# Two-layer attention kernel: three products of the context's values at other places in the first sequence's start

## What is computed

```python
def xattn(Q, K, V, valid_lens, Wq, Wk, Wv, Wo):
    q, k, v = heads(Q @ Wq), heads(K @ Wk), heads(V @ Wv)
    S = einsum('bhqd,bhkd->bhqk', q, k) / sqrt(dh)
    S = where(mask, S, -1e20)
    return merge(softmax(S) @ v) @ Wo

def ffn(h, ...):
    pooled = h.mean(axis=1)
    logits = relu(pooled @ gw1.T + gb1) @ gw2.T + gb2
    top_vals, top_idx = top_k(logits, 2); gates = softmax(top_vals)
    q, k, v = (svd_moe(h, p) for p in 'qkv')   # h @ Wm.T + experts + bias
    return svd_moe(merge(softmax(q k^T) @ v), 'o')

x = x + xattn(layernorm(x), ctx, ctx, lens, Wq, Wk, Wv, Wo)
x = x + ffn(layernorm(x), ...)
```

## Time and profile before

| | us |
|---|---|
| median of three runs | 1447.97 |
| lowest and highest | 1446.61, 1449.62 |
| profiled execution | 1451.72 |
| its span, first to last instruction | 1449.9 |
| its mean granted TensorE clock | 0.971 |

### The profile page before, as it was taken

One profiled execution on the slowest core, in us unless ns is written; L12 is line 12 of the kernel. 1 busy time (PEld: TensorE's weight loads), 2 busy tenths in 40 slices (PEclk: granted clock), 3 DMA queues, 4 the chain that ended last, 5 costly groups with the idle time before them and its releaser, 6 DMA issues.

```text
span 1449.9 us, 17120 instructions
## 1 busy us (share of the span) xinstructions
PE 1397.0 (96%) x5688; PEld 700.9 (48%) x5688; DVE 952.5 (66%) x1687; ACT 862.0 (59%) x1499; POOL 681.1 (47%) x411
## 2 busy tenths in 40 slices
PE   6999999999999999999999999999999999899886
PEld 4545544544454554545455554545455554444332
DVE  4464577767766777767766777767767676766532
ACT  2426474866487664866578663866577663756441
POOL 2022143556455462546446462545446462567463
PEclk9989989999999999999999999999999999999967
DMA  6533233522533224522523224522423222422300
GB/s 213 155 108 95 50 69 102 136 74 49 141 80 91 71 58 116 150 75 45 136 76 104 70 57 118 150 74 45 125 83 103 74 54 80 132 59 55 77 28 29
DMA packets 78239, 130.81 MB, mean 90 GB/s; under 512 B 26358, under 2 KB 31094, under 8 KB 75079
## 3 DMA queue, kind: packets, MB, share of 16 engines
q1 hardware_dynamic: 74055, 128.66, 33.2%
q10 hardware_dynamic: 4096, 1.06, 0.3%
HBM read 66.08 MB, written 12.21 MB: 54 GB/s over the span
## 4 chain that ended last, share of the span: by engine, by line
PE 86%; ACT 5%; DMA 2%; issue 2%; POOL 2%; SPq 1%; DVE 1%; ACTq 0%; POOLq 0%; DVEq 0%
PE pj L1099 43%; PE scT L1184 9%; PE acc L1213 8%; PE sc L1156 7%; PE sc L1145 3%; PE pj L1129 2%; PE scT L1177 2%; PE pj L1193 2%; PE pj L1201 2%; PE pj L1222 2%; PE pj L1093 2%; ACT xhat L707 1%; PE pj L1074 1%; ACT qs L790 1%; PE pj L1085 1%
## 5 line engine op out<-in xcount | busy, mean ns | idle before, releaser
L822 ACT ACTIVATE probs<-scT 128x512 f32<-128x512 f32 x512 | 289.3, 594 | 315.3 <-PE scT L1184 311.3
L938 DVE TENSOR_REDUCE negmax<-sc 128x1 f32<-128x512 f32 x512 | 338.0, 684 | 148.8 <-PE sc L1156 148.0
L685 POOL TENSOR_TENSOR probs_sum<-probs_sum,probs 128x1024 f32<-128x1024 f32 x128 | 300.1, 2369 | 61.0 <-ACT probs L822 61.0
L1156 PE MATMUL sc<-ks,qs 96*128 96x512 f32 x512 | 262.6, 547 | 5.8 <-DMA ks<-ks 2.5
L965 DVE RECIPROCAL inv_sum<-pj 128x128 f32<-128x128 f32 x256 | 224.9, 921 | 64.2 <-PE pj L1222 26.2
L1184 PE MATMUL scT<-qs,ks 99*128 99x512 f32 x512 | 254.4, 526 | 8.4 <-ACT probs L822 5.6
L1099 PE MATMUL pj<-XT,Wqk 128*128 128x512 f32 x512 | 256.4, 597 | 0.0
L681 POOL TENSOR_TENSOR probs_sum<-probs 128x1024 f32<-128x1024 f32 x64 | 151.5, 2373 | 191.5 <-ACT probs L822 191.5
L1184 PEld LDWEIGHTS scT<-qs,ks 99*128 99x128 f32 x512 | 97.0, 195 | 130.5 <-ACT probs L822 62.1
L691 POOL TENSOR_TENSOR uv_stack<-UVS_sb,uv_stack 96x1024 fp32r<-96x1024 f32 x32 | 75.6, 2364 | 174.0 <-ACT UVS_sb L729 174.0
L1156 PEld LDWEIGHTS sc<-ks,qs 96*128 96x128 f32 x512 | 97.8, 193 | 96.8 <-issue 52.5
(11 more groups left out here) (101 smaller groups left out, 1723.0 us busy)
## 6 DMA issues: line engine op xcount, KB each, us to landing
Wqk<-in_WmT SPq DMA_DIRECT2D x16, 1024.0 KB, 8.0
Wvo<-in_WmT SPq DMA_DIRECT2D x16, 1024.0 KB, 5.7
UVS_sb<-in_UVS SPq DMA_DIRECT2D x64, 192.8 KB, 3.3
qs<-stage_lo SPq DMA_DIRECT2D x136, 64.0 KB, 2.3
qs<-qs SPq DMA_DIRECT2D x34, 256.0 KB, 3.1
X<-in_x SPq DMA_DIRECT2D x8, 1024.0 KB, 5.7
ks<-stage_lo SPq DMA_DIRECT2D x128, 64.0 KB, 2.0
ks<-ks SPq DMA_DIRECT2D x32, 256.0 KB, 3.0
```

Source lines behind the costliest of these rows:

```text
L685: nc.gpsimd.tensor_tensor(probs_sum[:, pair], probs_sum[:, pair], probs[:, kt % 2, pair], ALU.add)\
L822: nc.scalar.activation(probs[:, kt % 2, jj, :], scT[:, ST[step], :], ACT.Exp, scale=SCALE)\
L938: nc.vector.tensor_reduce(negmax[:, 0, n:n + 1], sc[:, SC[step], :], AX.X, ALU.max, negate=True)\
L1156: nc.tensor.matmul(sc[:, SC[step], :], qs[0:3 * DH, slot, jj, t * P:(t + 1) * P], ks[0:3 * DH, slot, jj, :], start=True, stop=True).then_i ...
```

## The change

Entries of the table `OWN` alone. Products 2, 3 and 4 move from times 61, 221 and 371 (behind `out1`, before the gate, and among the `q1` products of sequence 1) to -757, -575 and -449, between the jobs of sequence 0's cross attention. At the three old places stand fillers: 9 more ahead of the 5 that are there, 4, and 5. Two groups of fillers among the cross jobs go, of 1 and 4 matmuls. In all 45 filler matmuls instead of 32.

```diff
-    "context_values": {(0,): -2137, (1,): -1089, (2,): 61, (3,): 221, (4,): 371},
+    "context_values": {(0,): -2137, (1,): -1089, (2,): -757, (3,): -575, (4,): -449},
-    "warm": {(0, 2): -989, (1, 3): -909, (2, 1): -663, (3, 4): -423, (4, 5): 71, (5, 2): 170, (6, 3): 244, 
-        (7, 3): 323, (8, 2): 334, (9, 3): 555, (10, 4): 768},
+    "warm": {(0, 2): -989, (1, 3): -909, (2, 9): 61, (3, 5): 71, (4, 2): 170, (5, 4): 221, (6, 3): 244, (7, 3): 323,
+        (8, 2): 334, (9, 5): 371, (10, 3): 555, (11, 4): 768},
```

## The result

| | before | after |
|---|---|---|
| median, us | 1447.97 | 1454.5 |
| lowest and highest | 1446.61, 1449.62 | 1452.12, 1461.74 |
| profiled execution | 1451.72 | 1461.74 |
| its span | 1449.9 | 1460.0 |
| ratio of times (95% interval) | | 1.0053 (1.0032 to 1.0073) |

The changed kernel is slower by 6.5 us, 0.5%. The prediction had 1447.3 us and no change, with a range up to 1451.5: it was wrong, and the measured time lies above the range.

A forecast was written before the change was run, and what follows sets the result against it. TensorE, busy 96% of the span, was taken as the bound. Terms +0.7 - 0.55 - 2.31 + 1.5 gave -0.7 us: 1451.0 us by the profiled execution, 1447.3 by the median, range 1443.0 to 1451.5.

The forecast's parts named there:

- What bounds the kernel: Whole kernel: TensorE busy 96% of the span, so early wins or losses carry to the end nearly one for one.
- the products would hold it: Cross stage: dense work of the moved products keeps TensorE's granted clock at 1.00 from 66.5 to about 85 us.
- the shift's transfer behind the loads of `Wqk`: Job 3's shift, issued beside the loads: 0 taken, since 1.7 us of delay are free; full 5.9 would cost 2.4.
- the caught transfer: Rival, job 3's shift delayed behind Wqk loads: +2.4, +1.7 in all, 1449.7 us; idle time can add a fall; chance 0.14.
- The cross stage, +0.7: 64.4 to 90.59 us: 23.0 us of work plus 3.9 of waits, 26.9 against 26.2; bounds -3.2 and +2.8.
- Old place of product 2, 0: Behind out1: fourteen fillers, 3.15 us, lie in a 4.7 us wait for the layer norm, so no change.
- Old place of product 3, -0.55: Before the gate: gate's product moves from 114.24 to about 112.8; last transposition and first q1 gain 0.55 us.
- slower rival: At the gate: without product 3 the clock falls near 115; 5.5 us more there, 4.8 in all, 1452.8 us; chance 0.11.
- Old place of product 4, -2.31: Among q1 products: 3.43 us out, five fillers of 0.225 in; uv_stack ready half a microsecond before the first weff.
- a thing that would prove it wrong: At the first weff: the prediction is wrong if TensorE waits there for uv_stack.
- The clock fall at 87: Behind product 4: one short fall, ended by out1 products, costing +1.5 us, from 0 to 3.5.
- the mark of being wrong: Between 60 and 130 us: the prediction is wrong if the clock is 0.50 for over 7 us.

The follow-up runs named there:

- e10: The changed kernel run again, unaltered; ratio to the kernel before 1.0061 (1.0046 to 1.0076).
- e7: e6 with product 4 moved to time 61, behind out1, in place of the fillers there; ratio to the kernel before 0.9999 (0.9982 to 1.0015).
- e9: Kernel before with product 4 alone moved, to time -757, fillers at other places, Wqk loads first; ratio 1.0015 (0.9999 to 1.0030).
- e11: The same kernel as e7, run on another chip; ratio to the kernel before 1.0003 (0.9992 to 1.0015).
- e1: Changed kernel with the two Wqk loads put ahead of the products' stores; ratio to the kernel before 1.0033 (1.0021 to 1.0046).
- e4: Changed kernel with six fillers behind product 4, loads left as changed; ratio to the kernel before 1.0036 (1.0020 to 1.0051).
- e5: Changed kernel with both edits, Wqk loads first and six fillers behind product 4; ratio to the kernel before 1.0012 (0.9994 to 1.0029).
- e6: Changed kernel with Wqk loads first, six fillers behind product 4, nine at the gate; ratio to the kernel before 1.0015 (1.0000 to 1.0030).
- e2: Changed kernel with nine fillers instead of four at product 3's old place; ratio to the kernel before 1.0044 (1.0027 to 1.0060).
- e3: Changed kernel with product 3 back at its old place, its four fillers removed; ratio to the kernel before 1.0067 (1.0043 to 1.0091).
- e12: The kernel before run again, unaltered; ratio 1.0000 (0.9983 to 1.0016).
- e8: Kernel before with 22 fillers instead of 5 in the cross stage, products at their old places; ratio 0.9991 (0.9978 to 1.0004).

## Why the prediction was wrong, point by point

**What bounds the kernel: right for the loss, not shown for gains.** What was lost by 220 us was still lost at the end: +5.5 in the first profile and +5.1 in e10 by the totals, +6.5 in the median. A gain by 220 us did not come through in the same way (e7, e9, e11). That TensorE's clock in the third slice was the thing to look at was right too, and so was the claim that the products would hold it: 1.00 from 66.0 to 85.9.

**The failing step: the shift's transfer behind the loads of `Wqk`, priced at 0.** The sum took 0 between the ends 0 and 2.4; the caught transfer was a rival with a chance of 0.14. The transfer issued at 83.84 took 5.74 us, nearly the 5.9 of the earlier trace rows. The reason given for 0 was that the shift "starts level with the loads and not two microseconds behind them"; issues at 83.29 and 83.84 beside loads at 83.34 and 83.77, with landings 4.3 and 5.7 us later, show that level is nearly as bad as behind. The only rows near that case were those of the earlier trace rows, at the upper end; that end should have been the forecast.

The square of e1, e4 and e5 sizes the two costs of that place, each over e5's 29.52, and the cut at `csT` parts them. In the changed kernel `csT` starts 2.05 us later than in e5, by the wait for the transfer, where the sum had 0 and the rival 2.4. Behind `csT` the half clock costs 1.5, as the sum had it. Together that is +3.5; the rival, which had both, came to 3.9. So the rival named the mechanism and nearly both prices.

What the prediction had no case for is the overlap. The clock fell at 86.0, ahead of `cden` and `cpv`, and what that costs (1.33 up to `csT` in e1) lay under the wait for the transfer. The fall alone (e1) is thus +3.0 and not +1.5, near the upper bound of 3.5 that the text gave. The transfer alone (e4) is +3.5, since its idle time brought a fall of its own, which the rival had as "the idle time can add a fall". The costs lie over each other and do not add.

**The cross stage, +0.7: too small by 1.7 even with the cures.** e6 has neither fall nor caught transfer and is at +2.4. The terms that were mis-sized: the three products took 3.65, 3.43 and 3.61, not 3 x 3.43 (+0.4); four of the six `cpv` and `cden` took 0.99 to 1.07 instead of 0.86 (+0.7); eight score records took 1.01 once instead of 0.82 (+0.2). That is 1.3; the other 0.4 lies in waits that I didn't assign. The largest wait, behind product 4, was right: 3.45 us foreseen to the next `cden`, 3.49 measured (82.22 to 85.71):

```profile
85.71 1.74 PE L1201 MATMUL pj<-probs,ones 77*32 77x512 f32 x8 [1.58 <-ACT probs L811]
87.15 2.01 PE L1193 MATMUL pj<-probs,V 77*32 77x512 f32 x8
89.62 1.14 PE L1177 MATMUL scT<-qsc,keys 99*77 99x512 f32 x2 [0.47 <-DMA qsc<-shift]
```

The chain of copy, split, issue and exponential from the earlier trace rows was the part of the working that held best. `csT` shows only 0.47 us of wait for the shift since `cden` and `cpv` at half clock cover the rest: the reason that e1 gained so little.

**Old place of product 2, 0: right.** The first transposition stands at 4.70 behind the residual in every kernel. e7 against e6 gives the other half of it: the product that no longer fills that wait costs 3.8 us in the stage.

**Old place of product 3, -0.55: the step right, its cover not.** The gate's product is 1.22 us earlier, where the prediction had 1.4 to 1.5, and q1 0.5 earlier in e2 and e6. In the changed kernel it is 0.54 later, for the clock fell at 120.1:

```profile
113.03 2.04 PE L1093 MATMUL pj<-ident_sb,xhat 128*128 128x128 f32 x12 [1.61 <-ACT xhat L707]
...
118.33 1.02 PE L1231 MATMUL pj<-pooled,gw1T_sb 128*128 128x1 f32 x8 [1.25 <-DVE pooled L993]
```

This is the prediction's slower rival, at its place but small: it was priced at 5.5 us and took 1.04 of q1, and in e10 and e1, where the fall was half as long, 0.05 and 0.16. The Trainium skill, page "TensorE: Matmul & The Clock Gate", Part 4 (PE-mode transpose), holds that transpositions don't engage the full clock; the traces agree in part: the fall came in a stretch of transpositions and one-column products, but with five fillers more the clock held 1.00 through the same transpositions in three executions of four (e2, e6, e11, and not e7).

**Old place of product 4, -2.31: too large.** The first weff is 1.75 us earlier, not 2.86. TensorE waits for `uv_stack` as soon as the q1 products aren't late by the clock (0.65 in e10, 0.55 in e6, 1.23 in e3), which the prediction had named as a thing that would prove it wrong. Half a microsecond of cover was thought to be there by asking for the experts' rows 1.4 us earlier. In e6 and e10 they were asked for 1.2 earlier, but SyncE's second issue, the last that the first `uv_stack` needs, came 0.97 us behind the first instead of 0.56 and took 3.5 and 3.6 us to land instead of 3.1, so that `uv_stack` was ready only 0.4 and 0.25 us earlier than in the kernel before.

**The clock fall at 87: right** in place, a microsecond early; its length, 6.8 us, just under the 7 us that the text set as the mark of being wrong. It came in the work that was named: `csT`, a wait, `cden` and `cpv`. The Trainium skill, page "TensorE: Matmul & The Clock Gate", Part 1 (The HAM clock gate), lets idleness take the clock. Two falls speak against idleness as the one cause: that of the earlier trace rows, where TensorE was busy 11.74 of 11.90 us ahead of it, and its repetition in e12, at 65.5 with 11.74 of 11.90 us again. The fall at 86.0 had a wait of 1.58 us ahead of it and can't tell the two apart.

**The sum.** By the terms measured: +5.94 in the stage, then -1.36 (third group of weff against the residual, 40.78 against 42.14) and +0.96 on to the denominators of self attention, with the fall at 144 in it: +5.5, against -0.7 foreseen. Of the 6.2 us between them, 3.7 are in the stage (2.0 the pair over the 1.5 that was in the sum, 1.7 the sizes), 1.5 in the two old places, and 1.0 behind. The median's +6.5 is 1.0 more than this sum, which no term here explains.

**Range and chances.** The caught transfer alone stood at 1449.7, inside the range; what it left out was the same case with the other terms at their bounds. The stage at its bound (+2.8 instead of +0.7) and the fall at its own (+3.5 instead of +1.5) add 4.1 to that: 1453.8, within 0.7 us of what was measured. Several terms that all had their slack on the same side were widened one at a time.

## What to carry to other kernels

Work that is moved from a wait that it filled into a stretch that is full costs its whole length, and the only thing that can pay for it there is the clock; here 22 fillers instead of 5 shortened the stage by 3.3 us, while three products of 3.4 to 3.65 us each could not be paid back. Where two costs fall on the same few microseconds, work out the time with each and with both, for they can hide each other, and an experiment that cures one may show next to nothing. When stores are put ahead of large loads on a queue, look at what the loads will now start beside: a transfer on another engine's queue that was alone before. Moving the loads again only changes which transfer is caught; what helps is to let them catch one that nobody waits for. And where one execution shows the clock held or lost by a few fillers, look at a second one of the same kernel before taking it as a rule.

## What the runs showed of the hardware

- A small transfer on ScalarE's queue issued within 0.1 us of two loads of `Wqk` on SyncE's queue landed in 4.3 to 5.7 us (after; 4.5 to 5.8 in e4, 4.7 to 6.3 in e2), nearly as late as one issued 2 us behind them (5.4 to 5.9). One issued 4.3 us behind the first of them and its second half 0.6 us later still took 5.1 and 5.9 us (e1; 4.9 and 5.4 in e9), while the loads themselves took 6.1 and 9.4 us to land (e1). One issued 16 us behind them took 1.9 to 2.2 (e1).
- TensorE's granted clock fell to 0.50 behind 11.90 us of which the engine was busy for 11.74, with score tiles, turned score tiles, 32-column products and a few fillers in the last 8 of them, and it did so in both executions of the kernel before (66.5 and, in e12, 65.5). Eight 128-column fillers at each of two places, and six at a third, left one short fall of 3.5 us there (e8).
- Two executions of one kernel, with TensorE busy 8.79 of the 10 us ahead in both, differed in whether the clock fell at the gate (e7, 115.3 to 118.7, and e11, no fall).
- Four matmuls of 512 columns in f32 took 3.43 us behind some work and 3.61 or 3.65 behind other, at the same places of the program in after and e6, and four 32-column products 0.86 or 0.99 to 1.07, all at the full clock. What makes the difference was not tried.
- Of four issues of experts' rows on SyncE, the gaps of starts were 0.56, 0.96 and 0.50 us in the kernel before and e8, and 0.97, 0.57 and 0.50 in every kernel whose stores had moved. That would fit 0.4 us that stay at some place of SyncE's program and not at a certain issue; it was not tried.
